# Two weight reloads behind the first loads of pair rows: SP's program before the burst of a sandwich of attention and a 64-expert layer

## What is computed

```python
x = x + layernorm(attention(layernorm(x)))        # 16 heads, causal; scores from a 64-wide basis
h = layernorm(x).reshape(2048, 128)
rw = route(h)                                     # 64 experts in 8 groups, 8 chosen per token
expert_out = vmap(lambda gw, uw, dw: silu(h @ gw.T) * (h @ uw.T) @ dw.T)(Wg, Wu, Wd)   # 88 hidden
routed = einsum('eth,te->th', expert_out, rw)
x = x + layernorm(routed + shared_mlp(h))         # shared: 176 hidden
```

## Time and profile before

| what | us |
|---|---|
| median of three executions | 421.49 |
| lowest and highest of them | 420.11, 421.81 |
| span of the profiled execution | 451.5 |
| PE busy in it | 399.2 (88%) |
| DVE busy | 288.2 (64%) |
| ACT busy | 212.9 (47%) |
| POOL busy | 184.8 (41%) |
| mean granted clock of TensorE | 0.952 |

### The profile page before, as it was taken

How to read it: one execution, slowest core, us unless ns; L and a number is a source line. 1 busy time by engine, 2 the same in 40 slices (tenths; PEclk the granted TensorE clock), 3 DMA queues, 4 the chain that set the end, 5 groups by cost and what they waited for, 6 DMA issues and landing times.

```text
span 451.5 us, 7319 instructions
## 1 busy us (share of the span) xinstructions
PE 399.2 (88%) x2023; PEld 301.9 (67%) x2024; DVE 288.2 (64%) x761; ACT 212.9 (47%) x557; POOL 184.8 (41%) x242
## 2 busy tenths in 40 slices
PE   7889997789999969979999999999749979897784
PEld 5779775355665646646999999996526656564563
DVE  5756987854566635661666666546338867694884
ACT  3668884234234312322666666663144524453424
POOL 7574554666665456600000000004734747667001
PEclk9999996789999998996999999999969989999998
DMA  6369200011489866223666666542211313231001
GB/s 174 112 247 404 97 2 1 12 37 46 159 260 298 203 165 162 81 78 110 179 181 171 181 180 174 168 116 76 71 47 54 99 46 99 82 94 54 13 6 46
DMA packets 65467, 54.03 MB, mean 120 GB/s; under 512 B 7013, under 2 KB 61333, under 8 KB 65429
## 3 DMA queue, kind: packets, MB, share of 16 engines
q1 hardware_dynamic: 60469, 44.85, 33.3%
q0 software_dynamic: 4096, 8.40, 6.4%
q10 hardware_dynamic: 864, 0.33, 0.3%
HBM read 31.53 MB, written 22.02 MB: 119 GB/s over the span
## 4 chain that ended last, share of the span: by engine, by line
PE 67%; DVE 11%; another core or an unknown queue 7%; issue 5%; POOL 5%; ACT 3%; DMA 1%; POOLq 0%; DVEq 0%; SPq 0%; ACTq 0%
PE ps L1794 13%; PE ps L1967 9%; PE ps L1765 8%; PE ps L1767 8%; PE ps L1766 8%; PE ps L1992 6%; PE ps L1945 3%; PE ps L1979 3%; DVE up_w L1308 3%; DVE hid L1318 2%; PE ps L1717 2%; PE ps L1656 1%; PE ps L1705 1%; PE ps L1898 1%
## 5 line engine op out<-in xcount | busy, mean ns | idle before, releaser
L1765 PE MATMUL ps<-x_hi,w_hi 128*128 128x512 f32 (+1 forms) x184 | 98.3, 534 | 25.9 <-DVE hid L1318 24.4
L754 POOL DMA_INDIRECT picked<-pair_y,slots x64 | 62.9, 983 | 137.2 <-DMA pair_y<-pair_out 118.7
L1004 ACT ACTIVATE ps<-ps 128x512 f32<-128x512 f32 (+1 forms) x92 | 51.6, 564 | 137.0 <-PE ps L1767 78.5
L1308 DVE TENSOR_TENSOR up_w<-ps,route_w 128x512 f32<-128x512 f32 (+1 forms) x92 | 61.2, 665 | 73.4 <-remote 31.4
L1794 PE MATMUL ps<-hid,w_raw 128*128 128x512 f32 (+1 forms) x182 | 94.1, 600 | 0.6 <-DVE hid L1318 0.6
L743 POOL DMA_INDIRECT pair_x<-x_rows,slots x64 | 62.5, 977 | 39.5 <-issue 21.0
L1765 PEld LDWEIGHTS ps<-x_hi,w_hi 128*128 128x128 f32 x184 | 35.5, 193 | 62.8 <-issue 34.8
L1767 PE MATMUL ps<-x_hi,w_lo 128*128 128x512 f32 (+1 forms) x184 | 72.3, 393 | 0.0
L1766 PE MATMUL ps<-x_lo,w_hi 128*128 128x512 f32 (+1 forms) x184 | 71.9, 391 | 0.0
L1318 DVE TENSOR_TENSOR hid<-ps,up_w 128x512 f32<-128x512 f32 (+1 forms) x92 | 61.5, 668 | 6.0 <-issue 2.3
L1401 DVE COPY pair_ht<-ps 88x256 f32<-88x256 f32 x64 | 26.9, 421 | 37.4 <-PE ps L1979 30.8
(11 more groups left out here) (220 smaller groups left out, 586.1 us busy)
## 6 DMA issues: line engine op xcount, KB each, us to landing
w_raw<-in_w_experts SPq DMA_DIRECT2D x44, 192.0 KB
pair_x<-zero SPq DMA_DIRECT2D x16, 512.0 KB, 5.6
pair_in<-pair_x SPq DMA_DIRECT2D x32, 256.0 KB, 3.0
pair_y<-pair_out SPq DMA_DIRECT2D x64, 128.0 KB, 2.2
gu_w<-in_w_experts SPq DMA_DIRECT2D x22, 256.0 KB
down_w<-in_w_experts SPq DMA_DIRECT2D x16, 176.0 KB
pair_x<-x_rows,slots POOLq DMA_INDIRECT x64
picked<-pair_y,slots POOLq DMA_INDIRECT x64
```

The lines of the kernel that those rows point to most:

```text
L754: g.indirect_dma_start(picked[:, t % 3, k, :], None, pair_y, bass.IndirectOffsetOnAxis(ap=slots[:, t, k:k + 1], axis=0)).then_inc(s_pick[t ...
L1004: a.activation(bank, bank, ACT.Silu).then_inc(s_gated, 1)
L1308: v.tensor_tensor(up_w[:, k % 2, 0:w], ps[:, gate_bank(k) + 1, 0:w], route_w[:, group, 512 * dense_at(q) + lo:512 * dense_at(q) + lo + w], ...
L1765: t_.matmul(out_, hi, mhi, start=start, stop=False)
```

## The change

SP's program does the block of lines 635 to 640 at n = 25 instead of n = 27. The number of instructions stays the same on every engine. By the order of the instructions, the programs of PE, DVE, ACT and POOL are the same row for row.

```diff
             BEFORE = (BURST_AFTER + 3) * SETS
             for n in range(2 * SETS, BEFORE):
-                if n == BEFORE - 1:
+                if n == BEFORE - 3:
                     load_late(len(late))
                     for t in range(ST):
                         sp.wait_ge(s_scat[t], 16 * CHOSEN)
                     for g in range(4):
                         load_pairs(g)
                 reload(n)
```

## The result

The changed kernel takes 418.96 us (median of 20 executions, 414.85 to 421.19), the kernel before, in the same comparison, 421.35 us (20 executions, 419.78 to 425.7). The ratio is 0.9944 with a 95% interval from 0.9927 to 0.9961: faster by 2.4 us, 1.6 to 3.1 us by the interval. The forecast was 5.1 us. The time lies in the forecast's range, and less than half of the expected gain came. Ratios and intervals leave out executions more than 1.5% above the fastest one of their kernel (here the 421.19), medians do not.

The account below looks back on a forecast made before the run. PE was taken to bound the kernel, standing idle before the burst for late pair-row loads. From 421.5 us, 3.6 for the wait and 1.5 for the clock gave 416.4 us, range 414.5 to 420.2.

Parts of the forecast that it names:

- The mechanism around the burst: At the burst's start PE waits 3.64 us for pair-row loads standing behind reload n = 26; starting earlier ends the kernel equally earlier.
- The slack of the scatters: Before the burst: scattered rows land between 192.5 and 194.0 us, so the wait goes with 3.1 to 4.3 us to spare.
- the part on the four loads: SP issues them from 192.9 to 194.1 us on; PE can turn the first from 195.9 to 197.1, wants it at 200.20.
- The step from the span to the timed executions: Without the trace's disturbances PE reaches the burst 5.3 us earlier; 1.4 to 3.6 us of the wait go, 3.6 taken.
- The clock's term: Behind the idle time at the burst the lower clock costs 3.1 us; ends 0 and 3.1, half taken, 1.5 us.
- the prediction's sum for a vanished wait: Against the profiled execution: 3.6 us of wait plus 3.1 us of lower clock, 6.7 us, a span of 444.8 us.
- the scatters become the wait: Rival: PE comes 5.3 us earlier, the scatters do not, PE still waits 2.2 us; 420.1 us, or 419.1; chance 0.19.
- The rival of the clock: Rival: the wait at the burst goes but the clock gives nothing back; 417.9 us, 417.0 to 419.0 around it; chance 0.30.
- Nothing happens: Rival: another wait in SP's program holds the loads until 200 us, or timed executions never had the wait; 421.5; chance 0.04.
- slower: Rival: the lower clock moves into the burst's dense units, two stretches cost 6.4 us; 424.3 us; chance 0.05.
- The rule of the Trainium skill: The share of cold work differs between runs, so a forecast would leave out the trace's 3.1 us: 417.9 us.

Follow-up runs that it names:

- The second trace of before: The kernel before, unchanged, profiled a second time: one execution of 421.07 us, span 419.3 us.
- the first trace: The kernel before, unchanged, as profiled for the prediction: span 451.5 us.
- the earlier scatters: POOL waits for the tile before the last one, up to 16 scatters under way: on the changed kernel 413.31 us, on the kernel before 421.04 against 420.92.
- filling: Matmuls on constants ahead of PE's wait for pair rows: four in the kernel before, 417.17 us against 421.17; two in the changed kernel, 415.79 against 421.04.
- altered scatters: Changed kernel with the eighth tile's scatters left out (414.37 us), two tiles under way (413.31), or six memsets ahead of the last tile's scatters (420.82).

## Why the prediction was right or wrong

**The mechanism around the burst** was right. The idle time of 3.7 us in front of the burst was SP's doing in the kernel before; it is there in every trace of a kernel whose loads stand behind the reload n = 26. The reloads held back showed no cost (the kernel with four of them behind the scatters is as fast), and what is won at the burst's start arrives at the end: the rest of the kernel takes 218.7 to 219.1 us in five traces at the full clock, wherever the burst starts.

**The slack of the scatters** is the step that failed. In the part on the four loads the prediction had the wait of 3.64 us go "with 3.1 to 4.3 us to spare". That was true of the recorded execution alone. The step from the span to the timed executions had the ends 1.4 and 3.6 us, and took the upper one, because POOL's wait of 4.11 us against 2.19 us a tile later seemed part of the disturbance. It was not. The second trace of before, without the disturbance, has the same two waits, the first even longer:

```profile
169.98 0.96 POOL L743 DMA_INDIRECT pair_x<-x_rows,slots  x1 [4.72 <-DMA pair_x<-x_rows,slots]
...
181.98 0.96 POOL L743 DMA_INDIRECT pair_x<-x_rows,slots  x1 [2.02 <-DMA pair_x<-x_rows,slots]
```

POOL's waits for scatters sum to 23.6 us there, against 17.6 us and some put down to issue in the first. From the first scatter to the last it took 103.9 us in the first trace (85.8 to 189.7) and 105.4 us in the second. PE, without the disturbance, ended k = 5 at 193.61 us and not at 200.20. So PE gained and the scatters did not: in the seven traces behind the first that have them unaltered, the last one is issued at 188.7 to 191.5 us, against 189.74. What remained of the wait was 1.59 us, and 0.6 to 2.3 us in the other traces of the changed place. The term measured 3.8 - 1.6 = 2.2 us and not 3.6.

The lower end, 1.4 us, was nearer, and in part by luck. The prediction had the rows there at 194.0 us, 4.3 us after an issue at 189.74; they were there at 193.92, 2.38 us after an issue at 191.54. The 2.8 to 4.3 us of the earlier trace rows are the landings of SP's four loads; that trace gives none for the scatters in the stretch. Two errors of about 1.9 us cancelled. PE's arrival, put at 194.9 us, was 195.34 in the changed kernel and lies between 191.4 and 195.6 in the thirteen traces behind the first.

**The clock's term**, taken as half of 3.1 us, measured 2.6 - 2.0 = 0.6 us (1.1 us by the pieces). The whole cost was sized about right (2.6 against 3.1 us). The choice of half was not argued from the idle time that stays, since none was expected to stay. With 1.6 us of idle time left the clock still falls, and most of its cost stays. Where the idle time goes altogether, the full 2.6 us come back. So the prediction's sum for a vanished wait, 3.6 + 3.1 = 6.7 us, is close to what the change and the earlier scatters do together, 7.7 us (5.4 to 9.1).

Together 2.2 + 0.6 = 2.8 us, against 2.4 measured (1.6 to 3.1). Of the 2.7 us that are missing from the forecast, 1.4 are the wait and 0.9 the clock.

**The rivals.** What happened is the rival "the scatters become the wait": 420.1, or 419.1 with some of the clock's cost, for 418.96 measured. It had a chance of 0.19, and its sign came: an idle time of PE that is still ended by `pair_in`, with the scatters just landed. The rival of the clock expected the idle time to be gone and the clock low; the clock was low, but with an idle time in front. "Nothing happens" and "slower" did not show: inside the burst no trace has the lower clock behind the first units. The rule of the Trainium skill under "TensorE: Matmul & The Clock Gate" (Part 1), that the share of cold work differs from run to run, agrees with the traces in the early part of the kernel: the mean granted clock from 68 to 88 us is 0.66 in the first trace of before and 0.83 in the second, of the same kernel. At the burst it did not decide: the clock was low behind every one of the eight idle times of 1.6 us or more in the table, and the rests behind the five of 3.7 us or more agree within 1.3 us.

**An unexpected coupling.** PE's arrival at the burst goes with its early clock. Of the thirteen traces behind the first, the three with a granted clock of 0.66 from 68 to 88 us have the end of k = 5 at 195.3 to 195.6 us, the ten with 0.74 to 0.83 have it at 191.4 to 193.7. The scatters follow in part: the first is issued at 87.0 to 87.4 us in the three and at 84.8 to 86.3 in the ten, and in the changed place the last one has landed between 191.0 and 194.0 (the loads start right behind it; the kernels with altered scatters are left out). In the four traces of a changed place with neither filling nor altered scatters, the two early arrivals (191.8 and 193.0 us) wait 2.2 and 2.3 us, the two late ones (195.3 and 195.6) 1.6 and 0.6. So a PE that arrives early loses part of what it won before. This was seen in four traces and was not tested.

## What to carry to other kernels

A slack that is read from one trace holds for that execution. When the span of the profile and the median of the times differ by 7%, find what the trace has in excess, and ask of each engine apart whether it is moved by it: PE came 5 to 9 us earlier here, POOL's chain of scatters lasted as long as before, and a slack of 3 to 4 us turned into a shortage of 1.6. Ask too whose transfers a row of landings counts. When a transfer is moved ahead of a wait, the next condition in line decides the gain: measure when that one is met, and see whether the edit that makes it earlier (here one more tile of scatters under way) is worth nothing alone and three times the gain together.

## What the runs showed of the hardware

An idle time of TensorE of 1.6 us behind a long stretch of work was followed by the lower clock (0.54 and 0.61 in the stretches from 198 to 202 us), and one of 0.6 us was not. The length alone does not decide: in the first trace of before one of 3.29 us was not followed by it either. Matmuls on constants in place of the idle time kept the clock at 1.00, and alone made the kernel before faster by 1.3 to 4.6 us with the same wait. Eight more indirect transfers of POOL under way at a time removed 21 us of its waits for landings. The landing of transfers to and from `pair_x` had a median of 3.6 us there (80 to 186 us) and at most 5.2 us, against 3.4 and 4.3 us in the changed kernel, but POOL hardly waited for it any more.

What stays open is where the 32 us of the first profiled execution came from (a span of 451.5 against 419.3 us for the same kernel). DVE and ACT stood still in it with no releaser on this core, and the second trace of the same kernel has none of it; no other trace here has a span above 421 us.
